# Message layers of a graph network: plan loads on TensorE, the wait for messages, and unread products in the second layer

## The reference, cut to what matters

```python
# layer 0
messages = relu(concat([h[src], h[dst]]) @ W_msg + b_msg)
agg_sum = segment_sum(messages, dst, 50000)
counts = segment_sum(ones, dst, 50000)
# layer 1
norm = deg_inv_sqrt[src] * deg_inv_sqrt[dst]
aggregated = segment_sum(h[src] * norm[:, None], dst, 50000)
```

## Time and profile before

| what | us |
|---|---|
| median of three runs | 4822.12 |
| profiled execution, its own time | 4793.24 |
| its span, first to last instruction | 4791.4 |
| mean granted TensorE clock over the span | 0.649 |
| PE busy in the span | 3037.5 (63%) |
| DVE busy | 2708.5 (57%) |
| POOL busy | 2762.8 (58%) |
| ACT busy | 916.2 (19%) |
| layer 0's message stage | 640 to 1217 |
| layer 1's message stage | 1567 to 1898 |

### The profile page before, as it was taken

How to read it: one execution, slowest core, us unless ns; L and a number is a source line. 1 busy time by engine, 2 the same in 40 slices (tenths; PEclk the granted TensorE clock), 3 DMA queues, 4 the chain that set the end, 5 groups by cost and what they waited for, 6 DMA issues and landing times. The chain is left out here.

```text
span 4791.4 us, 53751 instructions
## 1 busy us (share of the span) xinstructions
PE 3037.5 (63%) x12326; PEld 1838.8 (38%) x12326; DVE 2708.5 (57%) x6253; ACT 916.2 (19%) x1645; POOL 2762.8 (58%) x2438
## 2 busy tenths in 40 slices
PE   3564745655797899664777657777646665555424
PEld 1222534544665687441222224545312222222113
DVE  7997742222457444675777727777745554444323
ACT  0332410000122000221222214334212221111100
POOL 0673057777111673446777678888157776877631
PEclk8876655555767555555555568787578887677655
DMA  6333621111455111542222244444111121333215
GB/s 255 79 71 121 268 82 24 24 24 23 114 158 152 34 26 25 177 177 87 41 41 43 35 72 91 107 87 105 65 45 36 37 38 30 32 28 30 24 14 109
DMA packets 337039, 363.11 MB, mean 76 GB/s; under 512 B 236961, under 2 KB 268843, under 8 KB 336864
## 3 DMA queue, kind: packets, MB, share of 16 engines
q1 hardware_dynamic: 219890, 261.52, 16.7%
q0 software_dynamic: 94096, 80.65, 13.9%
q10 hardware_dynamic: 22878, 18.95, 1.2%
HBM read 174.93 MB, written 201.00 MB: 78 GB/s over the span
## 5 line engine op out<-in xcount | busy, mean ns | idle before, releaser
L801 PE MATMUL e_ps<-e_msg,e_hot 128*128 x2408 | 571.4, 424 | 222.9 <-issue 213.0
L801 PEld LDWEIGHTS e_ps<-e_msg,e_hot 128*128 128x128 f32 x2408 | 530.1, 329 | 301.8 <-issue 301.8
L1767 POOL DMA_INDIRECT u_a<-attended,dst_end x392 | 489.3, 1248 | 149.9 <-issue 119.1
L2401 PE MATMUL d_pl<-d_hot,d_fields 128*65 128x512 f32 x712 | 479.8, 836 | 0.0
L774 DVE TENSOR_TENSOR sums<-e_ps,sums 128x455 f32 (+1 forms) x172 | 108.1, 628 | 557.2 <-PE e_ps L801 557.2
L719 POOL DMA_INDIRECT e_msg<-from_src,e_src x200 | 192.5, 962 | 286.2 <-DMA e_first<-lot_first 227.2
L2345 POOL DMA_INDIRECT flows<-d_out,d_end x160 | 263.6, 1648 | 107.1 <-issue 104.7
L1424 ACT ACTIVATE u_zt<-u_pt 128x256 f32<-128x256 f32 (+1 forms) x392 | 164.2, 433 | 840.4 <-PE u_pt L1319 838.8
L2056 POOL DMA_INDIRECT list<-s_rec,s_place x200 | 200.6, 1003 | 212.5 <-DVE s_place L1972 156.5
L2332 POOL DMA_INDIRECT d_near<-term,d_rec x196 | 191.0, 975 | 194.3 <-DMA d_rec<-list 135.1
L724 POOL DMA_INDIRECT e_msg<-h1d,e_src x200 | 204.9, 1025 | 120.3 <-issue 60.6
(11 more groups left out here) (383 smaller groups left out, 7249.3 us busy)
## 6 DMA issues: line engine op xcount, KB each, us to landing
x<-sums SPq DMA_DIRECT2D x28, 896.0 KB, 7.8
u_x<-x SPq DMA_DIRECT2D x28, 896.0 KB, 5.7
terms<-s_zeros SPq DMA_DIRECT2D x16, 812.5 KB
s_key_row<-src_key SPq DMA_DIRECT2D x50, 256.0 KB
term<-u_h SPq DMA_DIRECT2D x14, 910.0 KB, 3.7
flows<-s_zeros SPq DMA_DIRECT2D x14, 896.0 KB
n_x<-in_x SPq DMA_DIRECT2D x14, 896.0 KB
h<-n_h SPq DMA_DIRECT2D x14, 896.0 KB
```

The lines of the kernel that those rows point to most:

```text
L801: last = nc.tensor.matmul(to, hot[s][:, q, :], rows, start=False, stop=q == LOT - 1)
L1767: pool.indirect_dma_start(A[s][:, j, :], None, net.attended[:, :], bass.IndirectOffsetOnAxis(ap=net.dst_end[:, tile:tile + 1], axis=0)).th ...
L2401: last = nc.tensor.matmul(pl[0:WEIGHT + 1, :], fields[:, j, :], hot[:, j, :], start=j == 0, stop=j == J - 1)
```

## The change

PE loads seven numbers per group instead of fifteen. They are the blocks, multiplied beforehand by 65 (`CV1`, the columns of a block's messages in SBUF), so that they serve as offsets. Since block plus tile grows by one per item, a slot follows from the item's place q in the group and the blocks: 65 x (q - (block of q - first block)). To let one number serve both, PSUM slots are 65 columns apart in layer 1 as well, where 64 are used. The chunk count moves to SP: per group SP loads it, waits for `msg_ready` and raises `lot_ready`, for which PE waits with a constant. In layer 1 PE issues 16 unread products in front of the first group's products, and three behind every group's.

```diff
--- before.py
+++ after.py
@@ -34,6 +34,7 @@
 FAR = 1 << 17
 NEG = -1e30
 CV = C + NH
+CV1 = C + 1
 TILES = NP // P
 BLOCKS = EP // P
 HALF = BLOCKS // 2
@@ -351,12 +352,12 @@
                 for n, part in enumerate(parts):
                     wide = part.stop - part.start
                     nc.vector.scalar_tensor_tensor(lane_of[:, part], tile_of[:, part], float(-P), spread_dst[:, n, 0:wide], ALU.mult, ALU.add)
-                block_in, tile_in = (row[0:1, 0:LOTS * LOT].rearrange("o (g q) -> o g q", q=LOT) for row in (block_of, tile_of))
-                nc.vector.tensor_copy(lots[:, :, 0:LOT], block_in)
-                nc.vector.tensor_tensor(lots[:, :, LOT:2 * LOT], tile_in, tile_in[:, :, 0:1].to_broadcast([1, LOTS, LOT]), ALU.subtract)
+                block_in = block_of[0:1, 0:LOTS * LOT].rearrange("o (g q) -> o g q", q=LOT)
+                nc.vector.tensor_scalar(lots[:, :, 0:LOT], block_in, float(CV1), None, ALU.mult)
+                nc.vector.tensor_copy(lots[:, :, LOT:2 * LOT], block_in)
                 nc.vector.tensor_copy(first_of[:, :], tile_of[0:1, 0:ITEMS:LOT])
                 v.drain()
-                nc.vector.tensor_scalar(lots[:, :, CHUNK_AT + 1], lots[:, :, LOT - 1], 2, None, ALU.logical_shift_right)
+                nc.vector.tensor_scalar(lots[:, :, CHUNK_AT + 1], lots[:, :, 2 * LOT - 1], 2, None, ALU.logical_shift_right)
                 v.drain()
                 nc.vector.tensor_scalar(lots[:, :, CHUNK_AT], lots[:, :, CHUNK_AT + 1], 1.0, None, ALU.add)
                 v.drain()
@@ -651,13 +652,13 @@
                 step(None, at(0, LAST))
 
 
-def lot_items(nc, pe, plan, g):
-
-    row = plan[0:1, g * PLAN:g * PLAN + 2 * LOT]
-    _, at = nc.values_load_multi_w_load_instructions(row, engines=(nc.tensor.engine,), min_val=0, max_val=BLOCKS - 1,
-                                                     skip_runtime_bounds_check_because="the plan is clamped where it is made")
-    chunks = pe.value_load(plan[0:1, g * PLAN + CHUNK_AT:g * PLAN + CHUNK_AT + 1], min_val=1, max_val=CHUNKS)
-    return at[0:LOT], [u.with_bounds(min_val=0, max_val=LOT - 1) for u in at[LOT:2 * LOT]], chunks
+def lot_items(nc, plan, g):
+
+    row = plan[0:1, g * PLAN:g * PLAN + LOT]
+    _, rows = nc.values_load_multi_w_load_instructions(row, engines=(nc.tensor.engine,), min_val=0, max_val=CV1 * (BLOCKS - 1),
+                                                       skip_runtime_bounds_check_because="the plan is clamped where it is made")
+    slots = [0] + [(CV1 * q + rows[0] - r).with_bounds(min_val=0, max_val=CV1 * (LOT - 1)) for q, r in enumerate(rows)][1:]
+    return rows, slots
 
 
 def edge_sums(nc, net, layer, sums):
@@ -689,13 +690,14 @@
         hot = [sb(f"hot{s}", [P, LOT, P]) for s in range(2)]
         nothing = sb("nothing", [3, LOT * (C + 1)], BF16)
         ps = [ctx.enter_context(nc.psum_tensor(f"{n}ps{s}", [P, 512], F32)) for s in range(2)]
+        unread = ctx.enter_context(nc.psum_tensor(f"{n}unread", [P, 512], F32))
         if two:
             dst = sb("dst", [P, BLOCKS], I32)
             near = [sb(f"near{s}", [P, J, C]) for s in range(3)]
         AHEAD = 3 if two else 4
         gathered = [sem(f"gathered{s}") for s in range(AHEAD)]
-        names = ("loaded", "cleared", "added", "msg_ready", "hot_ready", "multiplied", "placed", "pe_turn")
-        loaded, cleared, added, msg_ready, hot_ready, multiplied, placed, pe_turn = map(sem, names)
+        names = ("loaded", "cleared", "added", "msg_ready", "hot_ready", "multiplied", "placed", "lot_ready", "pe_turn")
+        loaded, cleared, added, msg_ready, hot_ready, multiplied, placed, lot_ready, pe_turn = map(sem, names)
         n_loads = 6 if two else 5
         with nc.Block() as block:
             @block.sync
@@ -707,6 +709,11 @@
                 sp.dma_start(numbers[:, :], net.dram["c_iota"][:, 0:P]).then_inc(loaded, 16)
                 sp.dma_start(plan[:, :], net.lot_plan[:, :]).then_inc(loaded, 16)
                 sp.dma_start(first[:, :], net.lot_first[:, :]).then_inc(loaded, 16)
+                sp.wait_ge(loaded, 16 * n_loads)
+                for g in range(LOTS):
+                    chunks = sp.value_load(plan[0:1, g * PLAN + CHUNK_AT:g * PLAN + CHUNK_AT + 1], min_val=1, max_val=CHUNKS)
+                    sp.wait_ge(msg_ready, chunks)
+                    sp.sem_inc(lot_ready, 1)
 
             @block.gpsimd
             def _(pool):
@@ -771,7 +778,7 @@
                     tile = v.value_load(first[0:1, g:g + 1], min_val=0, max_val=PLACES - LOT)
                     here = sums[:, bass.ds(tile, LOT), 0:wide]
                     v.wait_ge(multiplied, g + 1)
-                    nc.vector.tensor_tensor(here, ps[s][:, 0:LOT * wide].rearrange("p (u c) -> p u c", c=wide), here, ALU.add)
+                    nc.vector.tensor_tensor(here, ps[s][:, 0:LOT * CV1].rearrange("p (u c) -> p u c", c=CV1)[:, :, 0:wide], here, ALU.add)
                     v.drain()
                     v.sem_inc(placed, 1)
                 one_hots(0, 0, True)
@@ -785,23 +792,27 @@
             def _(pe):
                 pe.wait_ge(loaded, 16 * n_loads)
                 pe.wait_ge(cleared, 1)
-                blocks, slots, chunks = lot_items(nc, pe, plan, 0)
+                blocks, slots = lot_items(nc, plan, 0)
                 for g in range(LOTS):
                     s = g % 2
                     pe.wait_ge(placed, g + 1)
-                    nc.tensor.matmul(ps[s][:, 0:LOT * wide], net.ones3[:, :], nothing[:, 0:LOT * wide], start=True, stop=False)
+                    nc.tensor.matmul(ps[s][:, 0:LOT * CV1], net.ones3[:, :], nothing[:, :], start=True, stop=False)
                     pe.wait_ge(hot_ready, g + 1)
-                    pe.wait_ge(msg_ready, chunks)
+                    pe.wait_ge(lot_ready, g + 1)
                     pe.sem_inc(pe_turn, 1)
-                    by_slot = ps[s][:, 0:LOT * wide].rearrange("p (u c) -> p u c", c=wide)
+                    if g == 0 and not two:
+                        fill(nc, net, unread, 16)
                     now = zip(blocks, slots)
+                    all_rows = msg[:, :, :].rearrange("p b c -> p (b c)")
                     for q, (b, u) in enumerate(now):
-                        rows = msg[:, bass.ds(b, 1), 0:wide].rearrange("p b c -> p (b c)")
-                        to = by_slot[:, bass.ds(u, 1), :].rearrange("p u c -> p (u c)")
+                        rows = all_rows[:, bass.ds(b, wide)]
+                        to = ps[s][:, bass.ds(u, wide)]
                         last = nc.tensor.matmul(to, hot[s][:, q, :], rows, start=False, stop=q == LOT - 1)
                         if q == LOT - 2 and g + 1 < LOTS:
-                            blocks, slots, chunks = lot_items(nc, pe, plan, g + 1)
+                            blocks, slots = lot_items(nc, plan, g + 1)
                     last.then_inc(multiplied, 1)
+                    if not two:
+                        fill(nc, net, unread, 3)
 
 
 def attention_sums(nc, net):
```

## The result

The changed kernel takes 4909.5 us (median of four runs, 4907.96 to 4910.85), the kernel before 4823.3: a ratio of 1.0178, 95% interval 1.0161 to 1.0196, so 86 us slower. The profiled execution after took 4910.46 us, span 4908.6, mean granted clock 0.634.

A forecast was written before the change was run, and what follows sets the result against it. PE at half clock was taken to bound the second message layer. A clock fall after ten groups adds 92 us, the small parts change nothing; put on the 4822.1 us median this gives 4914 us, range 4826 to 4942.

The forecast's parts named there:

- the bound: Second message layer: PE sets the pace, busy 314.8 of 316.0 us at granted clock 0.50, 3.66 us a group.
- the price of an unread product: Second layer: each costs 0.43 us at 1.2 GHz, so a group takes 4.94 us; 0.22 us each at full clock.
- The sum: Second layer: clock falls after ten groups, 76 groups at 4.94 us follow, last ends at 1987 instead of 1895: +92 us.
- The two edges given: Second layer: a clock fall after 6 or 14 groups instead of ten makes it +98 or +86 us.
- the start: Second layer: 16 unread products take 5.5 us and lift the clock; groups begin at 1584.4, 2.7 us each.
- it falls at a long gap: Second layer: PE catches up with its messages after 6 to 14 groups, waits, and loses the full clock; 0.75 us survived, 1.67 not.
- it stays down: Second layer: after the fall, three unread products in a row per group do not raise the clock; groups stay at 4.94 us.
- rival 2: Second layer: the clock falls and rises in turn; with half the groups cold +16 us, 4838 us; chance 0.08.
- The seven-number load: PE's sequencer, per group: seven numbers cost 0.78 us at 0.079 us each, making the new list about 2.4 us.
- stay within 2 us: First message layer: its time was to be unchanged within 2 us.
- the -0.4: Fewer loads on PE's sequencer: some 0.7 us per group less, nearly all hidden; taken as -0.4 us (0 to -2).
- rival 1: Second layer: the clock holds or returns as soon as there is a backlog; ends 45 us earlier, 4777 us; chance 0.19.

The follow-up runs named there:

- the late start: Changed kernel, but in the second layer PE begins its 16 unread products and first group only when 15 groups' messages have arrived: 4792.1 us, ratio 0.9936.
- The kernel with one gap: As the late start, but in the second layer group 40 waits for the messages of group 55: 4909.0 us, ratio 1.018.
- the version with 13 groups ahead: As the late start, but PE begins when 13 groups' messages have arrived instead of 15: 4783.0 us, ratio 0.9911.

## Why the prediction was right, point by point

**Right: the bound and the price of an unread product.** 4.947 us per slow group stands against the 4.94 predicted: three at 0.43 us on top of 3.66. The sum said +92 us for a fall after ten groups, the layer shows +87.4 for one after 13; by the same prices 13 give +85. The two edges given do not come out of those prices: at 4.94 - 2.7 us a group, 6 or 14 groups make +101 or +83 and not +98 or +86.

**Right: the start.** PE began its groups 13.0 us after the first gather, at 1599.88; forecast was 1584.4 on the clock of before, where the layer begins 15.3 us earlier, which is 12.9. The sixteen took 6.0 us up to the first product instead of 5.5, and the groups ran at 2.82 us in the mean (2.64 where nothing waits) against 2.7.

**Right: it falls at a long gap.** It fell in the 14th group where ten were taken and 6 to 14 allowed; the late start, which differs in that it begins late enough to have no gap, kept the clock. How long is too long stays as open as the earlier trace rows left it: 0.42 to 0.65 us in nearly every group did no harm (old loads, late start), 1.55 with 0.54 behind it did; with four in a row, 0.55 and then 0.90 us in one group was survived, and 0.54 and then 0.90 us another time was not.

**Right, by a weak argument: it stays down.** The kernel with one gap shows it. But the row leaned on, four in a row at 0.50 in the last update stage, bounds nothing: that stretch lasted 13 us, and with four per group the clock came back after 48 us and after 7. Three in a row happens to be the largest number tried that fails, which is luck. The prediction's rival 2 was one more unread product away and deserved more than 0.08.

The Trainium skill, "TensorE: Matmul & The Clock Gate", section "Why this matters for your kernels", would have the backlog heal the clock. Here 356.2 of 356.8 us busy at 0.50 speak against it, and so do the 304.0 of 304.0 us of the late start without the three: being busy, as the profile counts it, is not enough.

**Mis-sized, without effect on the time.** The seven-number load was to take 0.78 us by an equal price per number, and takes 1.057 (0.305 for one number, 1.337 for fourteen): the price per number is not equal, and the list is 2.6 us instead of 2.4, which is level with a fast group's 2.64 and no longer clearly below it. The net 0.7 us a group that the loads were to save came to some 0.5 where the list is the bound (45.1 us over 86 groups). At half clock it is hidden, as forecast.

**Wrong: the first layer does not stay within 2 us.** It took 582.2 to 582.6 us in all eleven kernels run with the new loads, and 575.2, 577.7 and 580.6 in the three with the old ones: 2 to 7 us more. Its 400 gathers took 1.011 to 1.012 us in the mean against 0.992 to 1.005, which is up to 8 us, and the traces show which: with the new loads 48 of them take over 1.0 us, with the old ones 21, 24 and 27, and every one of these starts inside a one-hot operation of VectorE (the last section has more on this). The prediction took the length of a gather as given. From the end of the last gather to the last eviction it takes 23.8 us with the new loads and 24.3 with the old ones, so the loads save there the 0.5 us that the -0.4 allowed for. Between the medians nothing of it can be seen (the kernel without unread products is level with before, in an interval of 9 us to either side).

**The prediction's rival 1** could be had, though not by itself: 4777 us was its price, and the version with 13 groups ahead takes 4783.

## What to carry to other kernels

Ask of any edit that makes an engine faster whether its supply keeps up; an engine that overtakes its supply stops, and here the stop took away the clock that the unread work had bought, while the unread work stayed to be paid at the slow price. Holding a clock and lifting it are two questions with two numbers: try the edit with a late start and with one gap on purpose. A shorter instruction list that shows nothing at one clock can be worth tens of microseconds at the other, so judge it where it is the bound.

## What the runs showed that was not expected

A faster PE slows the gathers that feed it. Time line of GpSimd's gathers and VectorE's one-hots in the changed kernel, where PE is fast and then where it is slow:

```profile
1616.05 1.09 DVE L774 TENSOR_TENSOR e_hot<-e_lane,e_numbers 128x896 f32<-128x896 f32 x1
1616.72 1.24 POOL L731 DMA_INDIRECT e_msg<-h1d,e_src  x1 [0.30 <-issue]
...
1619.16 1.09 DVE L774 TENSOR_TENSOR e_hot<-e_lane,e_numbers 128x896 f32<-128x896 f32 x1
1619.52 1.56 POOL L731 DMA_INDIRECT e_msg<-h1d,e_src  x1 [0.30 <-issue]
...
1666.91 0.94 POOL L731 DMA_INDIRECT e_msg<-h1d,e_src  x1 [0.30 <-issue]
1667.14 1.09 DVE L774 TENSOR_TENSOR e_hot<-e_lane,e_numbers 128x896 f32<-128x896 f32 x1
```

A gather that starts inside a one-hot operation (with 0.42 and 0.73 us of it still to run) takes 0.30 and 0.62 us longer than 0.94; one already under way when the operation starts (1666.91) does not. The traces of all 14 kernels bear this out for the second layer: of 2800 gathers 621 take over 1.0 us, each of these starts inside a one-hot operation with 0.21 to 1.05 us still to run and ends 0.81 to 0.85 us behind its end, and no other gather takes over 0.96. The gather of 1.85 us in the earlier trace rows, whose length the prediction took as given, started 0.07 us into such an operation. Where PE is fast through most of the layer, more gathers fall in this way, 78 in the late start against 18 before, though hardly more one-hot operations run while the gathers do (80 against 70): what changes is when they start. The mean of the layer's gathers is 0.999 us in the changed kernel, 1.063 in the version with 13 groups ahead, 1.175 with five unread per group and 1.218 with the old loads and a late start. The Trainium skill, "SBUF — State Buffer", section "Who interferes with whom", has a VectorE instruction with two SBUF inputs contend with a GpSimd instruction that reads SBUF; the rows agree in kind, as the gathers read `e_src` and the one-hots `e_lane` and `e_numbers`. A probe in the same section, in which `tensor_tensor` held up no DMA, does not fit them; for this kernel the rows decide. Doubling the operation ahead of each one-hot operation of the second layer, in the kernel without unread products, was to show its share:

```diff
+                    if not two:
+                        nc.vector.tensor_tensor(hot[s][:, :, :], lane[:, LOT * g:LOT * (g + 1)].unsqueeze(2).to_broadcast([P, LOT, P]),
+                                                numbers[:, :].unsqueeze(1).to_broadcast([P, LOT, P]), ALU.is_equal)
+                        v.drain()
```

> The changed kernel without unread products, and in the second layer VectorE builds each group's one-hots twice (the second time over the first). PE stays at half clock with groups 3.66 us apart, so only VectorE's share changes. Without the doubling a gather takes 1.02 us in the mean, 0.945 where no one-hot operation touches it. Theory (a gather is held up while VectorE runs the one-hot operation): the mean rises to 1.07 to 1.15, the last gather starts 12 to 35 us later after the first than the 263 without the doubling, and the time stays at 4818 to 4830, since PE is behind the messages by 54 us. Rival (gathers are slower because PE itself is faster): mean 1.00 to 1.03 as without the doubling.

```profile
L731 POOL DMA_INDIRECT e_msg<-h1d,e_src x200 | 208.0, 1040 | 124.3 <-DMA e_first<-lot_first 63.7 <-issue 60.7
```

The mean rose to 1.040 us, between the two expectations, and the last gather came 267.8 us after the first, 4.5 later. The doubling fell short because 143 one-hot operations ran while the gathers did, but only 21 gathers took over 1.0 us: how often a gather starts well inside an operation depends on how the two beats fall together, and not on the number of operations alone. The time, 4805.5 us (ratio 0.9969, 0.9942 to 0.9995), does not come from the edit: the layer takes 325.1 us, against 324.3 without the doubling, and the profiled difference lies behind it, in 2891.1 against 2914.6 us of untouched stages.
